# Weight folds and pointwise stage in one block: the folds between the evacuations of the first two images

## The reference

```python
y = jnp.einsum('bchw,oc->bohw', x, pw_w)
x_pw = bn(y, pw_g, pw_b, pw_m, pw_v) + x
out = bn(dwconv(x_pw, dwk_w), dwk_g, dwk_b, dwk_m, dwk_v)
out = out + bn(x_pw * dw1_w.reshape(1, -1, 1, 1), dw1_g, dw1_b, dw1_m, dw1_v)
return jax.nn.gelu(out, approximate=False)
```

## Time and profile before

| what | us |
|---|---|
| median of 3 runs | 5778.59 |
| lowest and highest run | 5777.19, 5783.18 |
| span of the profiled execution | 5771.5 |
| first matmul of the pointwise stage | 71.28 |
| last store of the stage landed, depthwise block begins | about 376.4 |

### The profile page before, as it was taken

How to read it: one execution, slowest core, us unless ns; L and a number is a source line. 1 busy time by engine, 2 the same in 40 slices (tenths; PEclk the granted TensorE clock), 3 DMA queues, 4 the chain that set the end, 5 groups by cost and what they waited for, 6 DMA issues and landing times. The chain is left out here.

```text
span 5771.5 us, 78482 instructions
## 1 busy us (share of the span) xinstructions
PE 4950.2 (86%) x23504; PEld 3918.4 (68%) x23504; DVE 3670.1 (64%) x5128; ACT 3642.4 (63%) x7348; POOL 3545.3 (61%) x2992
## 2 busy tenths in 40 slices
PE   5979999979976776867867764997999999999999
PEld 5969999967733443443444434776888888888888
DVE  4423333367759999999999994775555555555555
ACT  0017777746657877877878774665566656555555
POOL 0017777757769888889888883775444444444444
PEclk9989999989988888988988887998999999999999
DMA  6987777679930321313223116997223223223220
GB/s 166 265 211 194 189 195 187 172 193 264 254 93 12 93 57 45 82 44 77 68 57 79 45 34 156 254 268 179 57 57 90 56 56 90 56 56 75 71 56 24
DMA packets 388599, 674.51 MB, mean 117 GB/s; under 512 B 21117, under 2 KB 346702, under 8 KB 368910
## 3 DMA queue, kind: packets, MB, share of 16 engines
q1 hardware_dynamic: 334768, 514.71, 38.3%
q10 hardware_dynamic: 53522, 156.21, 7.2%
HBM read 437.00 MB, written 233.87 MB: 116 GB/s over the span
## 5 line engine op out<-in xcount | busy, mean ns | idle before, releaser
L1580 POOL TENSOR_TENSOR hidden_part<-hidden_whole,hidden_part 128x448 fp32r<-128x448 f32 x672 | 751.8, 1153 | 1024.2 <-ACT hidden_part L1545 1024.2
L676 POOL TENSOR_TENSOR omni_in_part<-omni_norm,omni_in_part 113x448 fp32r<-113x448 f32 x384 | 601.2, 1577 | 210.1 <-ACT omni_in_part L735 207.5
L1449 PE MATMUL f_out_ps<-hidden_part,ffn_wv_parts 128*128 128x448 f32 (+1 forms) x3360 | 720.2, 370 | 0.7 <-POOL hidden_part L1580 0.7
L1449 PEld LDWEIGHTS f_out_ps<-hidden_part,ffn_wv_parts 128*128 128x128 f32 (+1 forms) x3360 | 578.1, 177 | 103.1 <-POOL hidden_part L1580 35.2
L1623 DVE TENSOR_SCALAR hidden_whole<-f_hid_ps 128x448 f32<-128x448 f32 x672 | 417.5, 622 | 252.1 <-POOL hidden_part L1580 153.0
L87 PE MATMUL omni_ps<-omni_in_part,omni_band_part 113*112 113x448 f32 x1152 | 439.7, 382 | 111.1 <-POOL omni_in_part L676 78.4
L1050 PE MATMUL proj_ps<-mixT_low,kvr_weights_low 128*128 128x448 f32 x672 | 354.6, 612 | 205.5 <-ACT k_all L1114 161.3
L1235 POOL TENSOR_TENSOR input_times_v<-input_factor,v_all 128x448 f32<-128x448 f32 x336 | 420.1, 1250 | 159.4 <-ACT input_factor L1119 144.9
L1052 PE MATMUL proj_ps<-mixT_ends,kvr_weights_ends 128*128 128x448 f32 x1008 | 512.0, 591 | 0.0
L87 PE MATMUL dw_ps<-dw_in_part,dw_band_part 112*112 112x432 f32 (+3 forms) x1344 | 474.5, 353 | 42.1 <-POOL dw_in_part L477 42.1
L88 PE MATMUL dw_ps<-dw_in_part,dw_band_part 112*112 112x432 f32 (+3 forms) x1344 | 474.8, 353 | 0.0
(11 more groups left out here) (181 smaller groups left out, 13290.0 us busy)
## 6 DMA issues: line engine op xcount, KB each, us to landing
xin<-x SPq DMA_DIRECT2D x16, 2352.0 KB, 13.2
x_pointwise<-xp ACTq DMA_DIRECT2D x16, 2352.0 KB, 18.9
dw_in<-x_pointwise SPq DMA_DIRECT2D x24, 1568.0 KB, 24.4
y_gelu<-dw_out ACTq DMA_DIRECT2D x24, 1568.0 KB, 13.2
omni_in<-y_gelu SPq DMA_DIRECT2D x24, 1568.0 KB, 22.9
att_mix<-omni_out ACTq DMA_DIRECT2D x24, 1568.0 KB, 13.3
residual_pairs<-y_gelu SPq DMA_DIRECT2D x16, 2352.0 KB, 11.8
tok<-residual_pairs SPq DMA_DIRECT2D x16, 2352.0 KB, 9.0
```

The source lines that it names most:

```text
L676: pool.tensor_tensor(rounded(inner(p[1])), z[u][:, :, cc, :], inner(p[0]), ALU.subtract).then_inc(in_split, 1)
L1449: return pe.matmul(bank, rounded(w), rounded(x), start=start, stop=stop)
L1580: pool.tensor_tensor(rounded(kk[n % 2][1][:, h, :]), whole[h % KW][:, :], kk[n % 2][0][:, h, :], ALU.subtract).then_inc(kl_ready, 1)
```

## The change

`prepare` and `pointwise` become one block, `fold_and_project`. SP loads three tensors first: the four pointwise norm vectors (`pointwise_norm`, in place of `bcv`), the pointwise weights and the identity; then image 0, then the other small tensors with `gamma1` by itself, then image 1. VectorE folds the pointwise weights (on one vector of 192 instead of three), raises `folded`, for which TensorE waits, and then makes the evacuations of images 0 and 1 with the other folds between them. Image 0 takes the column folds after its second pair, the 13 x 13 filters after the fourth and fifth, the 5 x 5 filters after the next four, the output weights after the next three; image 1 takes scan, box and scaling. The bias of the 13 x 13 stage is folded by columns (96 x 2 values) and stored in two transfers. The memsets go to GpSimd. ScalarE stores images 0 and 1, then filters, tables and bias, and then the images from 2 on in a loop.

```diff
-def prepare(nc, ins, keep, wpw, shift_pw, f13_d, f5a_d, f5f_d, sa_d, sf_d, bias_d):
+def fold_and_project(nc, B, ins, keep, f13_d, f5a_d, f5f_d, sa_d, sf_d, bias_d, x, xpw_d):
...
+            for dst, src in [
+                (bpw[:, :, :], dram(ins["vecs"], 0, [[0, 128], [3 * C, 4], [1, C]])),
+                (wpw[:, :, :], ins["pw_wt"].rearrange("(k p) n -> p k n", p=CT)),
+                (keep.ident[:, :], ins["ident"]),
+            ]:
+                sp.dma_start(dst, src).then_inc(norm_loaded, 16)
+            load(0, 0)
...
+            totals["loads"] = n
+            load(1, 1)
...
         def _(pe):
+            pe.wait_ge(folded, 1)
...
+            pool.memset(f13[:, :, :], 0.0).then_inc(cleared, 1)
+            pool.memset(f5[:, :, :, :], 0.0).then_inc(cleared, 1)
+            pool.memset(run[:, :, :, 0:1], 0.0).then_inc(cleared, 1)
...
+            def fold_pointwise():
+                dve.wait_ge(norm_loaded, 48)
+                dve.tensor_scalar_add(sd[:, :], bpw[:, 0, :], BN_EPS).then_inc(norm_ready, 1)
+                dve.wait_ge(norm_root, 1)
+                link(dve.reciprocal(sd[:, :], sd[:, :]))
+                link(dve.tensor_mul(sd[:, :], bpw[:, 1, :], sd[:, :]))
+                for k in range(KT):
+                    link(dve.tensor_mul(wpw[:, k, :], wpw[:, k, :], sd[0:CT, :]))
+                    own = wpw[:, k, k * CT:(k + 1) * CT]
+                    link(dve.tensor_add(own, own, keep.ident[0:CT, 0:CT]))
+                dve.sem_inc(folded, 1)
+                link(dve.tensor_mul(sd[:, :], bpw[:, 3, :], sd[:, :]))
+                link(dve.tensor_sub(shift_pw[:, :], bpw[:, 2, :], sd[:, :]))
...
+            fold_pointwise()
+            for jp in range(PAIRS):
+                evacuate(None, 0, jp)
+                if jp == 1:
+                    fold_columns()
+                if jp in (3, 4):
+                    fold_large(jp - 3)
+                if 5 <= jp < 9:
+                    fold_small((jp - 5) // 2, (jp - 5) % 2)
+                if 9 <= jp < 12:
+                    fold_out_weights(jp - 9)
+            for jp in range(PAIRS):
+                evacuate(None, 1, jp)
+                s, k = jp // 3 // 2 % 2, jp // 3 % 2
+                if jp < 12:
+                    (scan_taps, box_taps, scale_taps)[jp % 3](s, k)
+                if jp == 12:
+                    sum_out_weights()
+                if jp == 13:
+                    dve.wait_ge(expo, 1)
+                    link(dve.tensor_scalar_add(keep.bonus[:, :, :], keep.bonus[:, :, :], -1.0))
...
             for u in range(2):
+                store(u, u, (u + 1) * PAIRS + NB)
+            act.wait_ge(step, totals["steps"])
+            act.dma_start(f13_d.rearrange("(k p) n -> p k n", p=CT), f13[:, :, :]).then_inc(filters_stored, 16)
+            act.dma_start(f5a_d.rearrange("(k p) n -> p k n", p=CT), f5[:, 0]).then_inc(filters_stored, 16)
+            act.dma_start(f5f_d.rearrange("(k p) n -> p k n", p=CT), f5[:, 1]).then_inc(filters_stored, 16)
+            act.dma_start(sa_d.rearrange("(k p) n -> p k n", p=CT), edge[:, 0]).then_inc(filters_stored, 16)
+            act.dma_start(sf_d.rearrange("(k p) n -> p k n", p=CT), edge[:, 1]).then_inc(filters_stored, 16)
+            for k in range(KT):
+                act.dma_start(dram(bias_d, k * CT, [[1, CT], [1, 1]]), bias[:, k:k + 1]).then_inc(filters_stored, 16)
```

More of the change, by code:

```diff
@@ L168, in prepare @@
         rates = m.sb("rates", [128, 2, 4])
+        xin = [m.sb(f"xin{u}", [CT, KT, HW]) for u in range(2)]
+        xp = [m.sb(f"xp{u}", [PXC, C, PJ]) for u in range(2)]
+        NB = 7
+        ps = [m.ps(f"pw_ps{i}") for i in range(NB)]
+        norm_loaded = m.sem("prep_norm_loaded")
         loads = m.sem("prep_loaded")
+        cleared = m.sem("prep_filters_cleared")
+        norm_ready = m.sem("prep_norm_variance")
+        norm_root = m.sem("prep_norm_root")
         var_ready = m.sem("prep_variances")
@@ L172, in prepare, with load @@
         step = m.sem("prep_steps")
+        folded = m.sem("pointwise_folded")
         expo = m.sem("prep_exponentials")
-        stored = m.sem("prep_stored")
+        filters_stored = m.sem("prep_stored")
+        loaded = [m.sem(f"x_loaded{u}") for u in range(2)]
+        ps_ready = m.sem("pw_product_ready")
+        ps_free = m.sem("pw_bank_free")
+        stored = [m.sem(f"xpw_stored{u}") for u in range(2)]
+        PAIRS = PJ // 2
         block = ctx.enter_context(nc.Block())
-        folds = [0]
+        totals = {}
         @block.sync
         def _(sp):
+            def load(b, u):
+                sp.dma_start(xin[u][:, :, :], dram(x, b * C * HW, [[HW, CT], [CT * HW, KT], [1, HW]])
+                             ).then_inc(loaded[u], 16)
+            for dst, src in [
[5 more added lines that the diff above has]
+            load(0, 0)
             n = 0
-            vecs = ins["vecs"]
             for dst, src in [
-                (bcv[:, :, :], dram(vecs, 0, [[0, 128], [1, NV * C]])),
                 (colv[:, :, :], ins["vec_cols"]),
                 (alph[:, :], dram(ins["alphas"], 0, [[0, CT], [1, 8]])),
[L186 to L190, removed]
                 (rates[:, :, :], ins["att_rates"]),
@@ L198, in _ @@
                 (w1[:, 1], ins["ffn_w1"]),
+                (gam[:, :], dram(ins["vecs"], V["gamma1"] * C, [[0, 128], [1, C]])),
+                (keep.w_low[:, :, :], ins["att_low"]),
+                (keep.w_end[:, :, :], ins["att_ends"]),
+                (keep.wo[:, :, 0:C], ins["att_out"]),
             ]:
@@ L345, in _ @@
                     for jp in range(PAIRS):
[L346 to L350 removed]
+                        evacuate(i, u, jp)
         @block.scalar
@@ L353, in _ @@
         def _(act):
-            for u in range(2):
-                act.sem_inc(stored[u], 16)
-            with act.Fori(0, B // 2) as i:
+            act.wait_ge(norm_ready, 1)
+            act.activation(sd[:, :], sd[:, :], ACT.Sqrt).then_inc(norm_root, 1)
+            act.wait_ge(var_ready, 1)
+            act.activation(cd[:, :, :], cd[:, :, :], ACT.Sqrt).then_inc(root, 1)
+            act.wait_ge(var_ready, 2)
+            act.activation(keep.bonus[:, :, :], uw[:, :, :], ACT.Exp).then_inc(expo, 1)
```

200 lines of the change are left out of this document (78 added, 122 removed).

## The result

| what | before | after |
|---|---|---|
| median, us (lowest to highest) | 5780.89 (5777.19 to 5785.06) | 5737.35 (5731.54 to 5746.31) |
| runs | 4 | 4 |
| span of the profiled execution, us | 5771.5 | 5744.5 |
| first matmul of the pointwise stage, us | 71.28 | 18.66 |
| first load of the depthwise block issued (`dw_in`), us | 378.68 | 343.16 |

A forecast was written before the change was run, and what follows sets the result against it. TensorE, busy 86% of a 5771.5 us span, bounds the kernel, leaving its idle start to gain. Start -54.4, pause +10.9 and clock +2.8 give -40.7 us, forecast 5737.9 us, own range 5732 to 5744, wide range 5723 to 5746.

The forecast's parts named there:

- What bounds it: Whole kernel: TensorE busy 86% of 5771.5 us, so a change at the start gains only TensorE's idle time there.
- The start: First matmul of the pointwise stage moves from 71.28 to 16.9 us, gaining 54.4 us, bounds 53.7 and 55.1.
- The folds among the evacuations: VectorE in images 0 and 1: folds hidden by seven banks, cost nothing, 1.1 us to spare, upper bound 3 us.
- rival (c): Images 1 or 3: VectorE's lag passes 7.2 us or store 1 misses its gap; 3 to 8 us more; chance 0.08.
- The pause: Image 4: moved filter stores delay the store of image 2, so TensorE waits 10.9 us once; bounds 3 us either way.
- The clock: After TensorE's pause: slow restart at the lower granted clock, costing 2.8 us.
- (a): Early images: filter stores cost nothing, slipping in beside loads; -54.4 us, total 5724 us; chance 0.12.
- (b): Load 4: q10 gets larger turns, x4 lands late, store 2 earlier; -45.9 us, total 5733 us; chance 0.05.
- (d): Later images: disturbed load-store cycle doesn't heal, stores miss in every second image; 64 us more, 5802 us; chance 0.03.
- (e): Start: TensorE held until all small loads are in, at 25 instead of 16.9; -32.6 us, 5746 us; chance 0.02.

The follow-up runs named there:

- no_narrow: Changed kernel with filter and table stores behind the store of image 14 and the bias turned by TensorE and stored as one row; 5726.50 us, ratio 0.9907.
- ident_split: no_narrow with only the identity's first 96 rows loaded ahead of image 0, the other 22 behind it; 5720.75 us, ratio 0.9902.
- scans_twice: no_narrow with each scan and box in image 1 made twice, as extra VectorE work; 5729.74 us, one run.
- bias_late: Changed kernel with only the two bias stores moved behind the store of image 14; 5734.69 us, ratio 0.9931.
- narrow_packed: no_narrow with 192 four-byte writes, side by side into a spare tensor, added behind the store of image 1; 5731.44 us, one run.
- after_again: The changed kernel profiled once more, nothing changed; 5736.93 us, one run.
- filters_late: Changed kernel with filter and table stores moved behind the store of image 14, bias stores left in place; 5736.09 us, ratio 0.9929.
- filters_late_bias_early: filters_late with the bias stores sent at 33.5 us, once image 1 has landed; 5727.76 us, ratio 0.9920.

## Why the prediction was right, and where not

**What bounds it.** Right. The idle start could be taken away, and where nothing else was lost it came through whole (no_narrow, 52.85 of 52.9 us). It could not be had by the load alone.

**The start: 54.4 forecast, 52.6 measured, 1.8 short and outside its bounds.** The step that failed is the landing of the first four loads: norm vectors "at about 5.5", image 0 at 16.9. The three small loads were priced by their bytes, at 289 GB/s. VectorE's timeline after shows that the last of them came at 8.20:

```profile
8.20 0.26 DVE L268 TENSOR_SCALAR sd<-pointwise_norm 128x192 f32<-128x192 f32 x1 [8.20 <-DMA identity<-ident]
...
24.16 0.56 DVE L338 TENSOR_TENSOR xp<-pw_ps,pointwise_shift 112x384 f32<-112x384 f32 x1 [1.92 <-PE pw_ps L245]
25.57 0.17 DVE L282 TENSOR_SCALAR cd<-colv 96x6 f32<-96x6 f32 x1 [0.85 <-DMA attention_out_weights<-att_out]
...
27.21 1.02 DVE L338 TENSOR_TENSOR xp<-pw_ps,pointwise_shift 112x384 f32<-112x384 f32 x2
```

The weights were ready at 12.0 instead of 9, still ahead of the image: what ended TensorE's wait was image 0, landing 16.5 us after its issue where 13.4 and 1.4 of queue ahead of it (at most 2.1) had been allowed. That the identity's load was slow is shown by ident_split; how much of the image's delay comes of it is open. Over the eleven profiles with this head the start lies between 17.9 and 19.8, each later than the forecast's latest, 17.6, and spread over more than the 1.4 us of its bounds.

**The folds among the evacuations: right.** The small loads landed at 25.6 (24.9), the third evacuation began at 27.21 (27.9), and the last one of image 1 at 61.80, with no pause of TensorE in that image. The lag was about half of what was forecast: 3.2 us behind TensorE's last matmul of image 1 (58.6), against 6.1, since VectorE had caught up by the end of image 0. scans_twice shows that the cover was real and what lies behind it: some 5 us. So rival (c) had the price right (3 to 8 us) and was not reached; its place would have been the start of image 2.

**The pause: one, in image 4, ended by the store of image 2, as forecast; 14.0 us instead of 10.9.** The mechanism of the sum was right and its size came out near for a reason that was not in it. Two steps failed, in opposite directions. "Load 4 is issued at 74.7 and holds the engines from 75.8" and "load 5 is issued at 92.9 and starts at 94.0" took a load to start 1.1 us after its issue; with q10 busy it takes about 4, which store 2 turned into an early start: bias_late has 7.5 us, near the lower bound of 10.9 - 3. And the bias was no term of its own. It was counted among the seven filter stores, by its bytes, which are nothing; its hold of the engines adds 6.5 us to the pause where the filters are there too, and makes 8.0 by itself. That the total came within 3.1 us of the forecast is luck: one error nearly paid for the other. Two stores that are moved are two stores to be priced, and the price was not in their bytes. The trace of before could not show it, for it has no such writes: there the bias went out as one row (`dw_bias<-sd`, 1x192, one packet of 768 bytes), and it is the change that folds it by columns and so writes it as 96x1 twice.

**The clock: 2.8 us.** What the stage lost beyond start and pause is 52.6 - 14.0 - 35.5 = 3.1. The granted clock is 0.54 in the pause and 0.50 in the six microseconds behind it, the 1.2 GHz level, as before at 366:377. no_narrow and narrow_packed differ by 13.4 us of stage at the same start, and by 7.1 of pauses: two restarts took 6.3, again 3.1 each. It isn't a constant: the same remainder (start gained, less pauses, less stage gained) is 2.7 us in after_again, 2.8 in filters_late, 1.7 in bias_late and 1.3 in filters_late_bias_early. In the last the half clock behind the pause ends sooner (22 matmul records in the six microseconds from 73 on, 19 in those from 118 on here), and how soon the clock rises after the first matmul differs as well.

**Sum.** -52.6 + 14.0 + 3.1 = -35.5, against -40.7: 1.8 us are the start's, 3.1 the pause's, 0.3 the clock's.

**Rivals.** (a), the filters for nothing, fell, though by less than it looks: with the bias out of the way store 2 missed load 5 by half a microsecond. (b), larger turns of q10, fell: in the pause the queues moved 104 and 106 packets, one for one, where the Trainium skill, "DMA: Bandwidth & Descriptors", Queues, rings and completion order, has 9 to 17 descriptors to a turn. (d), a cycle that doesn't heal, fell: behind the pause 1288 matmul records stand in one row, and no kernel of this study has a pause later than image 4. (e), a start at 25, fell by 18.66.

## What to carry to other kernels

When work is moved out of an idle stretch into a running one, price each transfer by what it does to the queue it is put into, above all the small ones: a bias of 768 bytes written from one partition per value cost as much as 2 MB of filters. Write such a vector as one row (turn it first, or fold it as a row, as the kernel before did), or put it behind the last load. In a cycle in which load and store fill the DMA engines, a store that is late by half a microsecond pays for a whole load; so move bulk stores behind the last load rather than between two. And read a stage at its own end, not in the whole time, when the rest of the program varies by more than the term in question.

By the whole time alone no_narrow cannot be told from the changed kernel (their intervals touch, 0.9890 to 0.9923 and 0.9917 to 0.9941); by the stage it is 17.3 us faster. The same holds of ident_split (0.9885 to 0.9918).

## What the runs showed of the hardware

- 192 writes of four bytes into 768 bytes side by side are over as packets in some 1 us but land over 6 to 9 us, with no other traffic too (312.9 to 320.4 in bias_late). What the DMA engines move in that time is slow: 47 to 86 GB/s in six kernels, a load's packet 3.9 us instead of 0.9. At 512 bytes apart they land in 1.2 us, and the stretch has 236 GB/s. With 384 writes the hold is hardly longer.
- A load issued while the other queue has much to do moves its first packet 3.1 to 4.0 us after the issue (76.81 to 80.77 in the changed kernel, 93.74 to 97.34 in bias_late), one issued when the other queue is nearly done 1.0 us; the busy queue meanwhile runs at 357 to 363 GB/s. What is worked off in that time was not tried.
- Two queues with work share the engines packet for packet, whatever the packets' sizes: 104 of 12544 bytes against 106 of 896.
- A load of 118 rows of 472 bytes, third in its queue, landed at 7.4 to 9.3 us in eleven profiles; cut to 96 rows, at 6.4 in one.
- Between equal starts of the same program TensorE's first matmul varies by some 2 us (17.9 to 19.8), and the 5.4 ms behind the stage by 15 us.
